# Token scales stored row by row, ternary pieces moved to later units, the second layer's first waits split, and the feed-forward stage run one tile further ahead

## The chip, the cores and the metric

The kernel runs on one core of one Trainium2 chip. What is measured is the device time of one execution, in microseconds (us). Engines are named PE (TensorE matmuls), DVE (VectorE), ACT (ScalarE), POOL (GpSimd) and SP (SyncE, which here only issues DMA transfers).

## The reference, cut

Two transformer layers, batch 4, 1024 tokens, width 512, 16 heads of 32:

```python
# layer 0: all in float32
h = sln(x, cond, ...); q, k, v = h @ Wqkv.T + bqkv
out = (softmax(q k^T) / 512**0.5 @ v) @ Wp.T + bp
h1 = out + x;  x1 = sln(h1, cond, ...) + h1
# layer 1: every linear is a "bitlinear"
act_quant(x):    s = 127 / clip(max|x| over the row); round(x*s) / s
weight_quant(w): s = 1 / clip(mean|w|); clip(round(w*s), -1, 1) / s
bitlinear(x, w, b) = act_quant(x) @ weight_quant(w).T + b
xn = rmsnorm(x1, g1) * (1 + scale) + shift         # scale, shift from bitlinear(c, w_ada1)
x2 = x1 + bitlinear(attention(bitlinear(xn, w_qkv)), w_proj)
h  = gelu(bitlinear(adaln(x2, ada2), w_fc1))
y  = x2 + bitlinear(h, w_fc2)
```

## The kernel before, in words

`build` runs three stages after each other, each with its own buffers, split by barriers: `layer0` (names a_...), `layer1a` (layer 1's attention, b_...) and `layer1b` (the feed-forward part, c_...). A batch is TT = 8 token tiles of 128 rows. Nothing is ordered by a scheduler: each engine's program is written out, and the engines meet at semaphores.

**layer0.** For a batch, PE makes q, k and v in 24 "units" of 512 columns (`UNITS`, 16 for q and k, v = 0 to 15, then 8 for v, 16 to 23), each four float32 products of 512 columns (L766), in four PSUM banks used in turn. From unit 8 (`PRE`) every unit also carries two chunks of the first heads' scores (L332), whose maxima DVE takes (L446, twice a unit). DVE's own part of a unit is the low half of q or k (L1032), or the value tile (L1039), which may be written only once all of the former batch's stored tiles have left their buffer (`s_qout`). Between these, for the batches 1 to 3, DVE does two further jobs, placed by unit number. The first is the former batch's input to layer 1: largest values, scales at unit 9 (`scales`, which makes the token scales `am1[:, 4, :]`, called dq), and eight-bit tiles at units 10 to 13 (`eight_bits`, L988). The second is a quarter of layer 1's ternary weights: `PIECES[b]` are 4 pieces of 2048 columns for batches 2 and 3, and 4 of 1536 and one of 2048 for batch 1; ACT rounds piece j at unit 9 + j (`ROUND_AT`), DVE clips it at unit 10 + j (`TERN_AT`, L1072 and L1074), POOL stores it. After the 24 units come the attention rounds, then a tail (projection, residual, norm). For the last batch scales and eight-bit tiles come after its tail, at the end of the stage.

SP's `quantized(b)` stores the eight tiles (L639), then dq by columns (L641) and dq by rows (L643). The last takes the 128 x 8 table and writes it as 1024 consecutive values, 4 bytes at a time.

**layer1a.** SP issues the loads of the first batch's tiles (xq), its dq (as rows and as columns), the weights w (qkv) and wp (proj), and the biases bqk and bv. w, wp and bqk share the semaphore `s_w`, and PE, ACT, POOL and DVE wait for all three before their first instruction. The first `work` (order `NEXT_ONLY`) transposes the tiles (kind X, four), then makes 16 units of q and k (kind QK). For each, DVE multiplies the product by dq (`dequantized`, L1464), ACT makes the high half (`high`, L1393), and DVE the low half (`low`, L1480), which waits for the high half. The low half follows its own `dequantized` at once for n < `EARLY` = 8. SP then reorders the first heads' q and k by DMA (L256), and DVE takes the first maxima (L446) of products on them.

**layer1b.** N = 32 token tiles go through a software pipeline: `steps` runs a list of (offset, function) for step n, each function on tile n + offset. Steps 1 to 24 run as a loop with four steps in its body, the others are written out before and behind it. A tile goes x_scale (ACT, L1705), modulate, shift, bias (POOL), maximum(0), clipped, inverse, factor (DVE, L1754, L1761, L1767, L1773), x_round (ACT, L1709), x_bits (DVE, L1778), x_transpose (PE, L1655), x_copy (ACT, L1713), fc1 (PE, L1664), hidden (DVE, L1789), gelu (ACT, L1719), maximum(1), clipped, inverse, factor (DVE), h_round (ACT, L1723), h_bits (DVE, L1795), h_transpose (PE, L1673), h_copy (ACT, L1728), fc2 (PE, L1683), residual (DVE, L1801).

## Time and profile before

| what | value |
|---|---|
| median of three runs | 3114.76 us (3105.6 to 3115.96) |
| the profiled execution | 3107.7 us |
| its span, first to last instruction | 3105.5 us |
| mean granted TensorE clock | 0.973 |
| busy: PE, DVE, POOL, ACT | 2840.1, 2244.1, 1999.2, 1788.0 us |

The program's stages, in us from the span's start:

| stretch | stage | PE busy | DVE busy | ACT busy |
|---|---|---|---|---|
| 415 to 506 | units of batch 1 | 87.68 | 60.74 | 32.46 |
| 792 to 884 | units of batch 2 | 87.12 | 59.39 | 31.87 |
| 1170 to 1263 | units of batch 3 | 87.56 | 59.38 | 31.87 |
| 1506 to 1585 | last tail, then eight-bit tiles and stores | 31.42 | 52.76 | 15.65 |
| 1585 to 1651 | layer1a's start | 37.71 | 38.77 | 20.71 |
| 1651 to 2778 | layer1a's attention | 1070.15 | 828.89 | 729.28 |
| 2778 to 3106 | layer1b | 268.46 | 270.56 | 244.75 |

The layer0 attention between these stretches makes up the rest. A stretch in which PE is busy nearly all the time can only be shortened by the little it idles; in the last tail, in layer1a's start and in layer1b it waits for others a good part of the time.

### The profile page before, as it was taken

The page shows a single profiled execution, that of the slowest core. Times are in us where ns is not written, and L with a number is a line of the kernel's source. Part 1 is how long each engine was busy: PE and PEld are TensorE (multiplying, and loading weights), DVE is VectorE, ACT ScalarE, POOL GpSimd, SP SyncE. Part 2 cuts the span into 40 slices and gives each one's busy share as a digit, 9 for nine tenths or more (in the row PEclk, how much of TensorE's full clock was granted, in tenths as well). Part 3 has the DMA queues.
Part 4 walks back from the last instruction along what each step waited for, and adds up shares of the span by engine and source line. Part 5 has one row for each costly group of instructions (what it writes and reads, how often), then busy time and mean ns, then how long its engine had stood idle before and what let it go on. Part 6 is the DMA issues. An engine that isn't in the chain of part 4 may idle for free. (4 is left out here: it accounts for less than half of the span.)

```text
span 3105.5 us, 69316 instructions
## 1 busy us (share of the span) xinstructions
PE 2840.1 (91%) x21927; PEld 1403.9 (45%) x21927; DVE 2244.1 (72%) x4442; ACT 1788.0 (58%) x3210; POOL 1999.2 (64%) x1674
## 2 busy tenths in 40 slices
PE   7999999999999989999739998999899899958898
PEld 5444444444444444445314444454444445524444
DVE  3677686776867777677647777776877687738997
ACT  2366553664546634466325666666666766657887
POOL 0288634886258852588526885888588778854341
PEclk9999999999999999999969999999999999979999
DMA  5022333223422324123031313221422232233000
GB/s 184 22 55 58 140 105 52 52 75 126 112 46 52 115 86 105 42 52 92 35 95 42 77 43 101 57 70 26 111 74 56 51 91 53 46 132 146 30 27 35
DMA packets 99769, 230.62 MB, mean 74 GB/s; under 512 B 22332, under 2 KB 28580, under 8 KB 97960
## 3 DMA queue, kind: packets, MB, share of 16 engines
q1 hardware_dynamic: 97816, 220.90, 25.2%
q0 software_dynamic: 1680, 6.33, 1.3%
q8 instruction: 141, 2.31, 0.3%
q14 instruction: 132, 1.08, 0.1%
HBM read 89.71 MB, written 35.73 MB: 40 GB/s over the span
## 5 line engine op out<-in xcount | busy, mean ns | idle before, releaser
L446 DVE TENSOR_REDUCE b_mxs<-ps 128x1 f32<-128x512 f32 x1024 | 635.4, 682 | 201.0 <-PE ps L332 199.8
L446 DVE TENSOR_REDUCE a_mxs<-ps 128x1 f32<-128x512 f32 x1024 | 635.4, 682 | 183.3 <-PE ps L332 181.9
L417 ACT ACTIVATE b_p<-ps 128x512 f32<-128x512 f32 x1024 | 533.9, 603 | 206.7 <-PE ps L346 201.9
L417 ACT ACTIVATE a_p<-ps 128x512 f32<-128x512 f32 x1024 | 530.6, 602 | 212.1 <-PE ps L346 206.8
L304 POOL TENSOR_TENSOR b_sum<-b_p 128x512 f32<-128x512 f32 x384 | 496.5, 1296 | 87.9 <-ACT b_p L417 87.3
L304 POOL TENSOR_TENSOR a_sum<-a_p 128x512 f32<-128x512 f32 x384 | 498.3, 1301 | 76.9 <-ACT a_p L417 76.8
L332 PE MATMUL ps<-b_k,b_q 96*128 96x512 f32 x1024 | 443.0, 436 | 32.8 <-DVE b_mxs L446 27.0
L332 PE MATMUL ps<-a_k,a_q 96*128 96x512 f32 x1024 | 443.3, 440 | 16.7 <-DVE a_mxs L446 13.2
L346 PE MATMUL ps<-b_q,b_k 98*128 98x512 f32 x1024 | 400.7, 426 | 13.2 <-ACT b_p L417 9.9
L346 PE MATMUL ps<-a_q,a_k 98*128 98x512 f32 x1024 | 397.8, 422 | 14.4 <-ACT a_p L417 14.4
L360 PE MATMUL ps<-a_p,a_vx 128*32 128x512 f32 x2048 | 372.2, 599 | 11.1 <-POOL a_sum L309 9.3
L360 PE MATMUL ps<-b_p,b_vx 128*32 128x512 f32 x2048 | 370.8, 601 | 0.6 <-POOL b_sum L309 0.4
L362 PE MATMUL ps<-a_sum,a_unit 128*32 128x512 f32 x768 | 370.2, 599 | 0.0
L362 PE MATMUL ps<-b_sum,b_unit 128*32 128x512 f32 x768 | 368.9, 601 | 0.0
L309 POOL TENSOR_TENSOR b_sum<-b_sum,b_p 128x512 f32<-128x512 f32 x256 | 328.8, 1284 | 37.5 <-POOL b_sum L304 18.1
L309 POOL TENSOR_TENSOR a_sum<-a_sum,a_p 128x512 f32<-128x512 f32 x256 | 329.4, 1287 | 35.5 <-POOL a_sum L304 16.0
L332 PEld LDWEIGHTS ps<-b_k,b_q 96*128 96x128 f32 x1024 | 198.1, 194 | 214.2 <-issue 104.9
L332 PEld LDWEIGHTS ps<-a_k,a_q 96*128 96x128 f32 x1024 | 194.2, 190 | 210.3 <-issue 121.3
L346 PEld LDWEIGHTS ps<-a_q,a_k 98*128 98x128 f32 x1024 | 192.0, 189 | 145.2 <-ACT a_p L417 98.1
L346 PEld LDWEIGHTS ps<-b_q,b_k 98*128 98x128 f32 x1024 | 194.8, 191 | 128.5 <-ACT b_p L417 84.9
L766 PE MATMUL ps<-a_hT,a_w 128*128 128x512 f32 x512 | 231.1, 604 | 8.4 <-DVE a_hT L919 8.4
L426 ACT ACTIVATE a_ots<-ps 128x512 f32<-128x512 f32 x128 | 76.4, 597 | 132.4 <-PE ps L362 131.9
(220 smaller groups left out, 3888.8 us busy)
## 6 DMA issues: line engine op xcount, KB each, us to landing
a_q<-a_qh SPq DMA_DIRECT2D x128, 128.0 KB, 2.3
a_k<-a_kh SPq DMA_DIRECT2D x128, 128.0 KB, 2.4
b_q<-b_qh SPq DMA_DIRECT2D x128, 128.0 KB, 2.4
b_k<-b_kh SPq DMA_DIRECT2D x128, 128.0 KB, 2.4
a_kl<-in_x SPq DMA_DIRECT2D x4, 2048.0 KB, 8.5
a_q<-a_ql SPq DMA_DIRECT2D x64, 128.0 KB, 2.3
a_k<-a_kl SPq DMA_DIRECT2D x64, 128.0 KB, 2.3
a_kh<-in_x SPq DMA_DIRECT2D x4, 2048.0 KB, 14.4
```

The lines of the kernel that those rows point to most:

```text
L304: pair = pool.tensor_tensor(tile, self.key_tile(u, kt), self.key_tile(u, kt + 1), ALU.add)
L309: pool.tensor_tensor(tile, tile, self.key_tile(u, kt + 2), ALU.add).then_inc(self.s_sum, 1)
L332: pe.matmul(self.mx[RING[at]], self.q[j][0:96, t * P:(t + 1) * P], self.k[j][0:96, half * HALF:(half + 1) * HALF], start=True, stop=True). ...
L346: pe.matmul(self.st[RING[at]], self.k[j][:, kt * P:(kt + 1) * P], self.q[j][:, u * HALF:(u + 1) * HALF], start=True, stop=True).then_inc(s ...
L360: pe.matmul(self.ot[u][HD * c:HD * (c + 1), :], self.vx[k % 2][:, kt, :], self.key_tile(u, kt), start=r == 0, stop=kt + 3 >= TT)
L362: pe.matmul(self.ot[u][3 * HD:4 * HD, :], self.ones[:, :], self.sum[:, at % self.NS, :], start=r == 0, stop=r == self.ROUNDS - 1).then_inc ...
L417: act.activation(self.key_tile(u, kt), self.st[RING[CHUNKS * (k % NJ) + n]], ACT.Exp, scale=self.scale).then_inc(self.s_exp, 1)
L426: act.activation(self.ots[:, u, :], self.ot[u], ACT.Copy).then_inc(self.s_ots, 1)
L446: dve.reduce_max(self.mxs[:, c:c + 1], self.mx[RING[CHUNKS * j + c]], axis=AX.X).then_inc(self.s_mxr, 1)
L766: mm = pe.matmul(ps[:, bank(v), :], lhs, rhs, start=k == 0, stop=k == KC - 1)
```

## The change

It has four parts.

1. **Rows of dq.** PE transposes the 128 x 8 table into a corner of a PSUM bank (`token_scales`, at unit 10 of the next batch, or after the last tail); DVE copies the 8 x 128 result out (`token_rows`, at unit 12, or after the last `scales`); SP stores it as eight rows of 512 bytes. SP waits for the copy ahead of this store. PE's m_transpose at unit 20, which uses the same bank, waits for the copy too.
2. **Later pieces.** In batches 1 to 3 a ternary piece j is rounded at unit 11 + j and clipped at unit 13 + j.
3. **First waits of layer1a.** bqk is loaded second, wp last and with a semaphore of its own, for which PE waits only before the first tail work. PE waits for w and bqk at the first QK product, not before its transposes; ACT at the first high half. In the first round the low half of unit n - 1 follows the dequantization of unit n.
4. **layer1b.** x_scale and POOL's three steps work on tile n + 6 instead of n + 5 while x_round and maximum(0) work on n + 5 (before: n + 4), so a tile has a step between x_scale and x_round. x_scale stands before x_round on ACT. x_bits works on tile n + 4 (before: n + 3) and stands later on DVE. The first x tile is loaded by itself, then the modulation rows and b2, then the other seven, then the weights.

```diff
-        SUM_AT, TOT_AT, INV_AT, ROUND_AT, TERN_AT = 1, 7, 8, 9, 10
+        SUM_AT, TOT_AT, INV_AT, ROUND_AT, TERN_AT = 1, 7, 8, (9, 11, 11, 11), (10, 13, 13, 13)
...
                     sp.dma_start(Pending.dq_col[b, :, :], am1[:, 4, :]).then_inc(s_qout, 16)
-                        sp.dma_start(Pending.dq_row[b, :].rearrange("(t p) -> p t", p=P), am1[:, 4, :]).then_inc(s_qout, 16)
+                    sp.wait_ge(s_dqrow, b + 1)
+                    sp.dma_start(Pending.dq_row[b, :].rearrange("(t p) -> t p", p=P), dq_t[:, :]).then_inc(s_qout, 16)
...
+                def token_scales(b):
+                    pe.wait_ge(s_dq, b + 1)
+                    pe.transpose(dq_ps, am1[:, 4, :], ident).then_inc(s_dqt, 1)
...
+                        if b and v == DQT_AT:
+                            token_scales(b - 1)
                         if v == MT:
                             pe.wait_ge(s_rowse, 1)
+                            if b:
+                                pe.wait_ge(s_dqrow, b)
...
+                def token_rows(b):
+                    dve.wait_ge(s_dqt, b + 1)
+                    if b:
+                        dve.wait_ge(s_qout, OUTS * b)
+                    dve.tensor_copy(dq_t[:, :], dq_ps).then_inc(s_dqrow, 1)
...
-                for dst, src in ((w[:, :, :], wq["qkv"]), (wp[:, :, :], wq["proj"]), (bqk[:, :], ins["b_qk"])):
+                for dst, src in ((w[:, :, :], wq["qkv"]), (bqk[:, :], ins["b_qk"])):
                     sp.dma_start(dst, src).then_inc(s_w, 16)
                 sp.dma_start(bv, rows(ins["b_v"], P)).then_inc(s_bv, 16)
+                sp.dma_start(wp[:, :, :], wq["proj"]).then_inc(s_wp, 16)
...
-                pe.wait_ge(s_w, 16 * 3)
...
+                        if kind == "QK" and n == 0:
+                            pe.wait_ge(s_w, 16 * 2)
...
-                            if kind == "QK" and n < EARLY:
-                                low(n, nxt)
+                            if kind == "QK" and 0 < n <= EARLY and tail is None:
+                                low(n - 1, nxt)
...
-    FIRST, AHEAD = -5, 5
+    FIRST, AHEAD = -6, 6
...
-                steps(pool, ((5, modulate), (5, shift), (5, bias)), all_mod)
+                steps(pool, ((6, modulate), (6, shift), (6, bias)), all_mod)
...
-                steps(act, ((-1, h_copy), (3, x_copy), (0, h_round), (1, gelu), (4, x_round), (5, x_scale)), all_x)
+                steps(act, ((-1, h_copy), (3, x_copy), (0, h_round), (1, gelu), (6, x_scale), (5, x_round)), all_x)
...
-                steps(dve, ((0, maximum(1)), (3, x_bits), (0, clipped(1)), (2, hidden(0)), (0, inverse(1)), (2, hidden(1)),
-                            (0, factor(1)), (4, maximum(0)), (0, h_bits), (4, clipped(0)), (-1, residual), (4, inverse(0)),
-                            (4, factor(0))))
+                steps(dve, ((0, maximum(1)), (0, clipped(1)), (0, inverse(1)), (2, hidden(0)), (2, hidden(1)),
+                            (0, factor(1)), (5, maximum(0)), (4, x_bits), (5, clipped(0)), (0, h_bits), (5, inverse(0)),
+                            (-1, residual), (5, factor(0))))
```

In the lists that follow, a row is one instruction (or several alike, x2): its line, its operation, its output and inputs.

DVE in layer0, units 9 (its end) to 11 of batch 1, before. a_kl and a_ql are a unit's low half, a_mxs its two maxima, a_vx and a_xv eight-bit tiles, a_p and a_sum a ternary piece:

```order
L1032 SCALAR_TENSOR_TENSOR a_kl<-ps,a_bqk,a_kh 128x512
L446 TENSOR_REDUCE a_mxs<-ps 128x1 x2
L988 TENSOR_SCALAR a_vx<-a_xv 128x512
L988 TENSOR_SCALAR a_xv<-a_xv 128x512
L1072 TENSOR_SCALAR a_p<-a_p 128x1536
L1074 TENSOR_SCALAR a_sum<-a_p 128x1536
L1032 SCALAR_TENSOR_TENSOR a_kl<-ps,a_bqk,a_kh 128x512
L446 TENSOR_REDUCE a_mxs<-ps 128x1 x2
L988 TENSOR_SCALAR a_xv<-a_xv 128x512 x2
L1072 TENSOR_SCALAR a_p<-a_p 128x1536
L1074 TENSOR_SCALAR a_p<-a_p 128x1536
```

The same engine after, units 11 to 13 of batch 1 (a_dq_t is the row copy):

```order
L1052 SCALAR_TENSOR_TENSOR a_ql<-ps,a_bqk,a_qh 128x512
L446 TENSOR_REDUCE a_mxs<-ps 128x1 x2
L1008 TENSOR_SCALAR a_xv<-a_xv 128x512 x2
L1002 COPY a_dq_t<-ps 8x128
L1052 SCALAR_TENSOR_TENSOR a_ql<-ps,a_bqk,a_qh 128x512
L446 TENSOR_REDUCE a_mxs<-ps 128x1 x2
L1008 TENSOR_SCALAR a_xv<-a_xv 128x512 x2
L1094 TENSOR_SCALAR a_p<-a_p 128x1536
L1096 TENSOR_SCALAR a_sum<-a_p 128x1536
```

The first ternary piece moved from the unit of the first eight-bit tiles to that of the last ones, and the small copy stands one unit ahead of it.

DVE at layer1a's start, before (b_qh<-ps is a dequantization, b_ql<-b_qh and b_kl<-b_ql a low half):

```order
L1464 TENSOR_TENSOR b_qh<-ps,b_dqr 128x512
L1480 SCALAR_TENSOR_TENSOR b_ql<-b_qh,b_bqk 128x512
L1464 TENSOR_TENSOR b_qh<-ps,b_dqr 128x512
L1480 SCALAR_TENSOR_TENSOR b_ql<-b_qh,b_bqk 128x512
L1464 TENSOR_TENSOR b_ql<-ps,b_dqr 128x512
L1480 SCALAR_TENSOR_TENSOR b_kl<-b_ql,b_bqk,b_kh 128x512
```

And after:

```order
L1492 TENSOR_TENSOR b_qh<-ps,b_dqr 128x512 x2
L1508 SCALAR_TENSOR_TENSOR b_ql<-b_qh,b_bqk 128x512
L1492 TENSOR_TENSOR b_ql<-ps,b_dqr 128x512
L1508 SCALAR_TENSOR_TENSOR b_ql<-b_qh,b_bqk 128x512
L1492 TENSOR_TENSOR b_ql<-ps,b_dqr 128x512
L1508 SCALAR_TENSOR_TENSOR b_kl<-b_ql,b_bqk,b_kh 128x512
```

Each low half now has the next unit's dequantization ahead of it.

One step of layer1b's loop on DVE, before (c_tk is a tile of x, c_h a tile of the hidden layer):

```order
L1754 TENSOR_REDUCE c_am<-c_h 128x1
L1778 TENSOR_SCALAR c_xq<-c_tk 128x512
L1761 TENSOR_SCALAR c_am<-c_am 128x1
L1789 SCALAR_TENSOR_TENSOR c_h<-ps,c_am,c_b 128x1024
L1767 RECIPROCAL c_am<-c_am 128x1
L1789 SCALAR_TENSOR_TENSOR c_h<-ps,c_am,c_b 128x1024
L1773 TENSOR_SCALAR c_am<-c_am,c_wsc 128x1
L1754 TENSOR_REDUCE c_am<-c_tk 128x1
L1795 TENSOR_SCALAR c_hq<-c_h 128x2048
L1761 TENSOR_SCALAR c_am<-c_am 128x1
L1801 SCALAR_TENSOR_TENSOR c_x<-ps,c_am,c_x 128x512
L1767 RECIPROCAL c_am<-c_am 128x1
```

And after:

```order
L1790 TENSOR_REDUCE c_am<-c_h 128x1
L1797 TENSOR_SCALAR c_am<-c_am 128x1
L1803 RECIPROCAL c_am<-c_am 128x1
L1825 SCALAR_TENSOR_TENSOR c_h<-ps,c_am,c_b 128x1024 x2
L1809 TENSOR_SCALAR c_am<-c_am,c_wsc 128x1
L1790 TENSOR_REDUCE c_am<-c_tk 128x1
L1814 TENSOR_SCALAR c_xq<-c_tk 128x512
L1797 TENSOR_SCALAR c_am<-c_am 128x1
L1831 TENSOR_SCALAR c_hq<-c_h 128x2048
L1803 RECIPROCAL c_am<-c_am 128x1
L1837 SCALAR_TENSOR_TENSOR c_x<-ps,c_am,c_x 128x512
L1809 TENSOR_SCALAR c_am<-c_am,c_wsc 128x1
```

The x bits moved from right behind the first maximum to behind the second, and three small operations on the hidden tile's maximum now follow each other instead of standing between long ones.

The same step on ACT, before and then after:

```order
L1728 ACTIVATE c_hT<-ps 128x1024 x2
L1713 ACTIVATE c_xqT<-ps 128x512
L1723 ACTIVATE c_h<-c_h,c_am 128x2048
L1719 ACTIVATE c_h<-c_h 128x1024 x2
L1709 ACTIVATE c_tk<-c_tk,c_am 128x512
L1705 ACTIVATE c_tk<-c_x,c_rs 128x512
```

```order
L1764 ACTIVATE c_hT<-ps 128x1024 x2
L1749 ACTIVATE c_xqT<-ps 128x512
L1759 ACTIVATE c_h<-c_h,c_am 128x2048
L1755 ACTIVATE c_h<-c_h 128x1024 x2
L1741 ACTIVATE c_tk<-c_x,c_rs 128x512
L1745 ACTIVATE c_tk<-c_tk,c_am 128x512
```

The scale of a later tile and the rounding of an earlier one changed places, and the rounding now stands right ahead of h_copy.

## Rows read from the trace of the kernel before

**Rows 1.** Timeline of PE, layer0: start, length, line, shapes; starts around units 8 and 22.

```profile
439.57 2.82 PE L766 MATMUL ps<-a_hT,a_w 128*128 128x512 f32 x6
...
498.16 1.02 PE L766 MATMUL ps<-a_w,a_hT 128*128 128x512 f32 x2
...
816.13 3.68 PE L766 MATMUL ps<-a_hT,a_w 128*128 128x512 f32 x8
...
872.67 3.60 PE L766 MATMUL ps<-a_w,a_hT 128*128 128x512 f32 x8
...
876.57 3.60 PE L766 MATMUL ps<-a_w,a_hT 128*128 128x512 f32 x8
...
1194.52 3.68 PE L766 MATMUL ps<-a_hT,a_w 128*128 128x512 f32 x8
...
1257.57 4.88 PE L766 MATMUL ps<-a_w,a_hT 128*128 128x512 f32 x11
```

**Rows 2.** Timeline of DVE, units of batch 2; brackets: idle before, what ended it.

```profile
834.07 0.74 DVE L1032 SCALAR_TENSOR_TENSOR a_kl<-ps,a_bqk,a_kh 128x512 fp32r<-128x512 f32 x1
...
836.79 1.22 DVE L1072 TENSOR_SCALAR a_p<-a_p 128x2048 f32<-128x2048 f32 x1
...
839.19 0.74 DVE L1032 SCALAR_TENSOR_TENSOR a_ql<-ps,a_bqk,a_qh 128x512 fp32r<-128x512 f32 x1
...
859.17 0.69 DVE L1039 TENSOR_TENSOR a_xv<-ps,a_bv 128x512 f32<-128x512 f32 x1 [5.33 <-DMA dq_row<-a_am]
```

**Rows 3.** DMA issues, 1555 to 1600 us: count, KB each, median us to landing.

```profile
xq<-a_xv SPq DMA_DIRECT2D x7, 128.0 KB, 1.9
...
dq_row<-a_am SPq DMA_DIRECT2D x1, 4.0 KB, 10.1
```

**Rows 4.** Timeline of SP's queue at layer1a's start: the issue of wp, bqk, first reordering loads.

```profile
1586.77 0.64 SPq L1279 DMA_DIRECT2D b_wp<-wq_proj  x1
1587.45 0.43 SPq L1279 DMA_DIRECT2D b_bqk<-in_b_qk  x1
...
1612.57 1.21 SPq L256 DMA_DIRECT2D b_q<-b_qh  x2
```

**Rows 5.** Timeline of PE, then POOL, at layer1a's start.

```profile
1597.77 3.57 PE L1325 MATMUL ps<-identb,b_kh 128*128 128x128 bf16 x32 [59.09 <-DMA b_bqk<-in_b_qk]
1602.73 5.34 PE L1337 MATMUL ps<-b_xqT,b_w 128*128 128x512 bf16 x24 [1.39 <-ACT b_xqT L1386]
...
1590.26 0.09 POOL L199 MEMSET b_fold<- 1x1 f32 x1
```

**Rows 6.** Timeline of DVE, layer1a's start: the first low half, the first maxima.

```profile
1605.34 0.75 DVE L1480 SCALAR_TENSOR_TENSOR b_ql<-b_qh,b_bqk 128x512 fp32r<-128x512 f32 x1 [0.79 <-ACT b_qh L1393]
...
1622.78 1.28 DVE L446 TENSOR_REDUCE b_mxs<-ps 128x1 f32<-128x512 f32 x2
```

**Rows 7.** Timelines of PE and of ACT, layer1b: one early tile, then the loop.

```profile
2820.89 1.06 PE L1673 MATMUL ps<-identb,c_hq 128*128 128x128 bf16 x16
...
2913.94 1.90 PE L1683 MATMUL ps<-c_w,c_hT 128*128 128x512 bf16 x8 [0.93 <-ACT c_hT L1728]
...
2921.08 1.06 PE L1673 MATMUL ps<-identb,c_hq 128*128 128x128 bf16 x16
...
2821.53 1.94 ACT L1728 ACTIVATE c_hT<-ps 128x1024 bf16<-128x1024 bf16 x2 [1.78 <-PE ps L1673]
...
2912.88 1.91 ACT L1728 ACTIVATE c_hT<-ps 128x1024 bf16<-128x1024 bf16 x2
...
2920.77 0.72 ACT L1709 ACTIVATE c_tk<-c_tk,c_am 128x512 f32<-128x512 f32 x1 [0.29 <-DVE c_am L1767]
```

**Rows 8.** x_bits and h_bits by tile, ns min/median/max; then POOL's timeline in the loop.

```profile
L1778 DVE TENSOR_SCALAR c_xq<-c_tk x32: 414/1018/1070, 2794.6 to 3069.0; 128x512 bf16<-128x512 f32 x32
...
L1795 DVE TENSOR_SCALAR c_hq<-c_h x32: 1226/1227/1228, 2816.7 to 3094.7; 128x2048 bf16<-128x2048 f32 x32
...
2922.32 1.26 POOL L1637 TENSOR_TENSOR c_tk<-c_tk,c_mod_r 128x512 f32<-128x512 f32 x1 [5.17 <-ACT c_tk L1705]
```

More of the change, by code:

```diff
@@ L641, in quantized @@
                     sp.dma_start(Pending.dq_col[b, :, :], am1[:, 4, :]).then_inc(s_qout, 16)
-                    with nc.allow_non_contiguous_dma(reason="1024 values a batch"):
-                        sp.dma_start(Pending.dq_row[b, :].rearrange("(t p) -> p t", p=P), am1[:, 4, :]).then_inc(s_qout, 16)
+                    sp.wait_ge(s_dqrow, b + 1)
+                    sp.dma_start(Pending.dq_row[b, :].rearrange("(t p) -> t p", p=P), dq_t[:, :]).then_inc(s_qout, 16)
                 def batch(b, last):
@@ L808, in batch @@
                         front(b + 1, b)
+                    else:
+                        pe.wait_ge(s_h1, TT * (b + 1))
+                        token_scales(b)
                 batches(pe, first, batch)
@@ L1141, in batch @@
                         chn.close()
+                        token_rows(b)
                         for t in range(TT):
@@ L1359, in work @@
                         pe.wait_ge(s_qf, UN * nxt + EARLY)
+                    if tail is not None:
+                        pe.wait_ge(s_wp, 16)
                     for kind, n, bank, before, part in order:
@@ L1389, in high @@
                     m, c = UNITS[n]
+                    if n == 0:
+                        act.wait_ge(s_w, 16 * 2)
                     act.wait_ge(s_qf, UN * nxt + n + 1)
@@ L1605, in _ @@
                 for b in range(B):
-                    sp.dma_start(x[:, TT * b:TT * (b + 1), :],
-                                 x_in[b * T:(b + 1) * T, :].rearrange("(t p) d -> p t d", p=P)).then_inc(s_x[b], 16)
-                    sp.dma_start(mod_r[:, b, :, :].rearrange("p i d -> p (i d)"),
-                                 rows(mod[b, :, :].rearrange("i d -> (i d)"), P)).then_inc(s_mod[b], 16)
-                    if b == 0:
-                        sp.dma_start(b2[:, :], rows(ins["b_fc2"], P)).then_inc(s_b2, 16)
+                    for lo, hi in ((0, 1), (1, TT)) if b == 0 else ((0, TT),):
+                        sp.dma_start(x[:, TT * b + lo:TT * b + hi, :],
+                                     x_in[b * T + lo * P:b * T + hi * P, :].rearrange("(t p) d -> p t d", p=P)).then_inc(s_x[b] if hi == TT else s_x0, 16)
+                        if (b, lo) == (0, 0):
+                            sp.dma_start(mod_r[:, b, :, :].rearrange("p i d -> p (i d)"),
+                                         rows(mod[b, :, :].rearrange("i d -> (i d)"), P)).then_inc(s_mod[b], 16)
+                            sp.dma_start(b2[:, :], rows(ins["b_fc2"], P)).then_inc(s_b2, 16)
+                    if b:
+                        sp.dma_start(mod_r[:, b, :, :].rearrange("p i d -> p (i d)"),
+                                     rows(mod[b, :, :].rearrange("i d -> (i d)"), P)).then_inc(s_mod[b], 16)
+                    else:
                         sp.dma_start(w1[:, :, :], wq["fc1"]).then_inc(s_w1, 16)
@@ L1695, in _ @@
                 act.wait_ge(s_rs, 1)
[L1696 removed]
+                act.wait_ge(s_x0, 16)
                 def all_x():
@@ L1702, in x_scale @@
                 def x_scale(n, r):
+                    if isinstance(n, int) and n == 1:
+                        act.wait_ge(s_x[0], 16)
                     if not isinstance(n, int) or n >= 2:
```

20 lines of the change are left out of this document (12 added, 8 removed).

## The prediction

> **What bounds the kernel now.** I read first the table of stages: PE is busy for nearly all of the attention and of layer0's units, and idles mainly in three places, the last tail with layer1a's start (1506 to 1651) and layer1b (268.46 of 328 us). The change touches these three and the units of the batches 1 to 3. Then I read the timelines there. In the units, PE runs one unit in 3.90 us when nothing holds it (872.67 to 876.57 [rows 1]); DVE needs 5.12 for a unit that carries a ternary piece of 2048 (834.07 to 839.19), 2.40 of it for the piece (836.79 to 839.19), and stands 5.33 before the first value tile until the row store of dq has landed [rows 2]. At the end of layer0 nothing runs but that store [rows 3]. At layer1a's start PE waits for the bias load [rows 5], and then DVE stands 0.79 before each low half until ACT has made the high half [rows 6]. In layer1b's loop PE idles 0.93 a tile before fc2, and ACT, which makes fc2's input, idles 0.29 before x_round for DVE's inverse [rows 7].
>
> About 0.3% of this time, 9.3 us, is what a measurement of this kernel can tell from no change; the chances use that bound.
>
> **Units of layer0 (parts 1 and 2).** From unit 8 to unit 22 PE took 439.57 to 498.16 = 58.6, 816.13 to 876.57 = 60.4 and 1194.52 to 1257.57 = 63.1 [rows 1]. Fourteen units at 3.90 are 54.6, so 4.0 + 5.8 + 8.5 = 18.3 are lost. Two things lose it: DVE's overloaded units (eight-bit tiles and a ternary piece in the same unit), and the wait for the store at unit 16. The store leaves after the last eight-bit tile and lands 10.1 after its issue, where a tile of 128 KB, written by rows, takes 1.9 [rows 3]. A store of eight 512-byte rows is no more work than that, so I take 1.9 and the wait of 5.33 goes, with its smaller or larger fellows in the other two batches. The bounds are 1.7 (the column store stands just below the tile's) and 10.1, where nothing would be gained; the last is a rival. The pieces now meet only one unit that has eight-bit tiles, unit 13, and then units 14 to 16 with nothing else. Unit 13 still takes 5.1 as in rows 2, and 14 and 15 take 5.12 less two eight-bit operations (about 0.4 each), 4.3. So 1.2 + 0.4 + 0.4 stay lost beyond 3.90, less what four banks of slack cover: I estimate 1.3 in each of the batches 2 and 3, none in batch 1 with its smaller pieces. Added are three transposes of 128 x 8 on PE: sixteen bf16 ones take 1.06 [rows 7], so 0.07 is the low end for one, and the first score chunk's 0.5 is more than one can take; I take 0.1, near the low end, as it is one small product, 0.4 in all with its wait. DVE's copy of 8 x 128 takes a small operation's time, beside a unit that has lost its ternary piece: nothing. If that cover were gone it would cost 0.2 to 0.7 (a low half) each. The new wait of PE at unit 20 is for a copy at unit 12: nothing. Queued behind SP's new wait is only the row store itself, and the wait ends at unit 12, while the last eight-bit tile, ahead of it in the queue, is made at unit 13. POOL's stores of the weights are issued two or three units later: DVE clips the last piece at unit 16 (17 in batch 1), POOL's attention work waits for the value tiles at 23, so nobody waits. The sum is 18.3 - 2.6 - 0.4 = **15.3**, between 10 (half of the overload stays) and 18.
>
> **End of layer0 (part 1).** The row store lands 10.1 after issue and layer1a starts behind it. With 1.9 it starts **8.2** earlier. The transpose and the copy there stand ahead of the first eight-bit tile on DVE, but those are paced by ACT's rounding, so they cost nothing or, without that cover, under 0.7. The bounds are 7 and 8.4.
>
> **layer1a's start (part 3).** PE began its transposes at 1597.77, released by the bias (issued 1587.45), and the first product at 1602.73, 4.96 later [rows 4, 5]. POOL's setup ends at 1590.35 [rows 5]; from there transposes and their copies put the first product at 1595.3. The bias, now issued where wp stood (1586.77, 0.68 earlier), would release PE at 1597.1, and wp's 512 KB no longer lie ahead of it, for which I take 0.9, half of what the transposes leave. That is 1596.2. The later decides: 1602.7 - 1596.2 = **6.5**, between 4 (nothing from wp's bytes, and the first products at the low clock, twice as long for their first 1.6) and 7.4 (the transposes decide). Behind it, DVE's low halves. From the first, 1605.34, to the first maxima, 1622.78, lie 17.4 with eight low halves, each behind an idle 0.79 [rows 6]. With the next dequantization between, the high half is ready. Eight by 0.79 is 6.3, less 0.2 for the first low half now one operation later: **6.1**. If instead the reordering loads set the time (issued 1612.57 [rows 4], after the fourth low half), only the first four count, 2.7.  I take the upper value, since the maxima come 10 us after those loads' issue, which no transfer in rows 3 takes when it has the queue to itself except the 4-byte one. Sum 12.6, between 7 and 14.
>
> **layer1b (part 4).** The period is 9.13 a tile: fc2 at 2913.94, h_transpose at 2921.08, its 1.06 and the idle 0.93 give the next fc2 at 2923.07. It closes through ACT: h_copy at 2912.88 to fc2 at 2913.94 is 1.06; fc2 to h_transpose, PE working without a gap, 2913.94 to 2921.08 is 7.14; and a copy that waits for its transposes starts 0.64 after them (2820.89 to 2821.53) [rows 7]. The sum is 8.84. In the loop the copy starts later than these 0.64, because x_round and x_scale stand ahead of it and x_round waited 0.29 for DVE. After the change x_scale, which waits for nobody in this step, fills that wait, so ACT's own loop is 9.13 - 0.29 = 8.84 too. Gain 0.29 x 24 loop steps = 7.0, with the steps written out around the loop about **7.3**. It needs DVE to be done in 8.84: its operations sum to about 8.1 with x_bits at the 0.41 that it takes away from POOL's stretch (its minimum, against a median of 1.02 [rows 8]), and with three dependent small operations in a row now, some 0.13 dearer each. The first tile alone makes the first x_scale earlier, but fc1 of tile 0 waits for w1, whose place in the queue hardly moved: 0 to 1. The bounds are 0 (a rival) and 12, should PE's 8.20 of own work set the period, 0.93 x 13.
>
> **Sum.** 15.3 + 8.2 + 12.6 + 7.3 = 43.4 off the profiled execution's 3107.7 (span 3105.5 and 2.2 around it) gives 3064.3. The median of the runs lies 7.1 above that execution; I add half, since runs of either kind occur: **3067.8**.
>
> **Rivals.**
> *The feed-forward period stays (0.15).* DVE's chain of dependent small operations, or x_round now right ahead of h_copy and behind an inverse that DVE makes after h_bits, takes the place of the wait removed. Against it: 0.7 us of slack on DVE. Then 7.3 is missing, or up to 6 more (0.25 a step) is lost: 3075 to 3081.
> *layer1a's start gains little (0.12).* Weights land no earlier, and the loads set the maxima: 4 + 2.7 instead of 12.6, 3073.7. For it speaks that transfers there share the engines.
> *The row store is no quicker (0.04).* Then 8.2 and about 7.5 of the units' gain are missing: 3083.5. Against it: both tile and column stores take under 2.
> *Slower (0.02).* h_bits, 1.227 us in every tile now [rows 8], falls into POOL's stretch of three operations. x_bits, which lies in it, takes 1.02 against 0.41, 2.5 times as long; h_bits would take 3.0, 1.8 more, and DVE, at 8.1 + 1.8 = 9.9, becomes the bound: 0.8 a step over 9.13, in 31 steps 24, and if residual and hidden are pushed into that stretch behind it 51. The latter costs more than all the gains: 3119. It decides if POOL's stretch starts some 2.4 us later against h_bits than its place behind x_scale says; x_scale follows two gelu operations of 1 us each on ACT, so it starts when h_bits has ended. This is the weakest of the cases.
> The Trainium skill, in "SBUF — State Buffer", section "Who interferes with whom", states that DVE and GpSimd contend only for a shared port pair, as an exclusive lock. By that the later engine waits out at most one instruction of the other, and the time lost doesn't grow with the length of its own. The rows above can't tell lock from slowing: 0.6 lost beside a POOL operation of 1.26 [rows 8] fits both. By the lock the overlap would cost at most one such operation a step, 1.27 x 31 = 39, and this rival would end at about 3107, no longer slower; I give that outcome 0.01.
>
> **Chances.** The forecast as it stands 0.66, the rivals as given (0.15, 0.12, 0.04, 0.02, 0.01). Faster by over 0.3% is all but the last two: 0.96, with 0.02 for no change and 0.02 for slower. The range takes the first three rivals' middle in and the unknown costs above: low 3054 (units 18, end 8.4, start 14, layer1b 9, and a median run equal to the profiled one), high 3084.
>
> **What would show it.** In the changed profile: PE units 8 to 22 in 54.6 to 57; no wait of DVE for dq_row before the value tiles; the row store landing in about 1.9; PE's first product in layer1a some 15 us earlier in the span than the units' gain alone says, and the first maxima about 14 after it, where it was 20; in the loop of layer1b a period of 8.84, x_bits at 0.41 and h_bits still at 1.227. The forecast is wrong if a transfer at layer1a's start takes longer because its neighbours moved, or if x_round waits for DVE in the loop again.

## The result, and the profile after

The changed kernel ran in 3070.38 us (median of four, 3068.01 to 3078.25), the kernel before in 3113.95 (four, 3105.6 to 3115.96). The ratio is 0.9869, 95% interval 0.9844 to 0.9895. A second series on one chip gave 0.9877 (0.9858 to 0.9895). 3067.8 had been forecast.

The profiled execution of the changed kernel is its slowest, 3078.25 us with a span of 3076.5; that of before was a quick one of its kind, 3107.7 us with a span of 3105.5. So between the two traces lie only 29.0, between the medians 43.6: the one lies 7.9 above its median, the other 6.3 below. The time is therefore followed below by stages.

The page's busy times after:

```profile
PE 2852.6 (93%) x21931; PEld 1415.0 (46%) x21931; DVE 2239.3 (73%) x4446; ACT 1791.2 (58%) x3210; POOL 1998.3 (65%) x1674
```

**Units of layer0.** PE's timeline in batch 2, the starts of units 8 and 22, and between them the only piece where it still waits (start, length, line, shapes, idle before and what ended it):

```profile
813.08 3.68 PE L773 MATMUL ps<-a_hT,a_w 128*128 128x512 f32 x8
...
852.77 0.50 PE L332 MATMUL ps<-a_k,a_q 96*128 96x512 f32 x1 [0.47 <-DVE a_mxs L446]
...
869.11 7.03 PE L773 MATMUL ps<-a_w,a_hT 128*128 128x512 f32 x16
```

They answer to [rows 1]: 56.0 where it was 60.4. Batch 1 takes 55.0 (58.6 before), batch 3 56.1 (63.1). DVE's first value tile no longer waits for a store, against 5.33 in [rows 2]:

```profile
851.44 0.68 DVE L1059 TENSOR_TENSOR a_xv<-ps,a_bv 128x512 f32<-128x512 f32 x1
```

**End of layer0, start of layer1a.** SP's queue: the row store, and the next stage's first load 2.92 behind it, where a store alone took 10.1 to land [rows 3]; then the first reordering load.

```profile
1561.44 0.34 SPq L646 DMA_DIRECT2D dq_row<-a_dq_t  x1
1564.36 0.35 SPq L1272 DMA_DIRECT2D b_kh<-xq  x1
...
1566.37 0.44 SPq L1302 DMA_DIRECT2D b_bqk<-in_b_qk  x1
...
1584.48 1.20 SPq L256 DMA_DIRECT2D b_q<-b_qh  x2
```

PE there, answering to [rows 5]: its transposes are released by POOL's setup, its first product by the bias, and the first score chunk now waits for a reordering load.

```profile
1570.53 3.57 PE L1348 MATMUL ps<-identb,b_kh 128*128 128x128 bf16 x32 [15.07 <-POOL b_fold L199]
1575.69 10.47 PE L1362 MATMUL ps<-b_xqT,b_w 128*128 128x512 bf16 x40 [1.58 <-DMA b_bqk<-in_b_qk]
...
1590.06 1.22 PE L332 MATMUL ps<-b_k,b_q 96*128 96x512 f32 x2 [2.69 <-DMA b_k<-b_kh]
```

DVE, answering to [rows 6]: the first low half has no idle before it, and the first maxima come 15.2 after the first product, where it was 20.05 (1602.73 to 1622.78).

```profile
1579.89 0.74 DVE L1508 SCALAR_TENSOR_TENSOR b_ql<-b_qh,b_bqk 128x512 fp32r<-128x512 f32 x1
...
1590.89 1.29 DVE L446 TENSOR_REDUCE b_mxs<-ps 128x1 f32<-128x512 f32 x2 [0.24 <-PE ps L332]
```

**layer1b.** One step of the loop on PE, answering to [rows 7]:

```profile
2889.66 1.90 PE L1717 MATMUL ps<-c_w,c_hT 128*128 128x512 bf16 x8 [0.67 <-ACT c_hT L1764]
...
2896.80 1.06 PE L1707 MATMUL ps<-identb,c_hq 128*128 128x128 bf16 x16
2898.53 1.90 PE L1717 MATMUL ps<-c_w,c_hT 128*128 128x512 bf16 x8 [0.67 <-ACT c_hT L1764]
```

And x_bits by its tile (ns minimum/median/maximum), answering to [rows 8]:

```profile
L1814 DVE TENSOR_SCALAR c_xq<-c_tk x32: 412/416/869, 2772.2 to 3034.6; 128x512 bf16<-128x512 f32 x32
```

The period is 8.87, where it was 9.13, and PE's idle before fc2 is 0.67 instead of 0.93.

### The profile page after: what moved, and what is told of

It reads as the page before. It is cut to its first block and busy times, and to the rows that moved or that the text cites. A ratio compares the mean times of both kernels' runs of the same rounds, so it can differ in the third digit from the quotient of the medians.

```text
span 3076.5 us, 69328 instructions
## 1 busy us (share of the span) xinstructions
PE 2852.6 (93%) x21931; PEld 1415.0 (46%) x21931; DVE 2239.3 (73%) x4446; ACT 1791.2 (58%) x3210; POOL 1998.3 (65%) x1674
```

## The experiments

All kernels are compared stage by stage in their traces, since single executions of one kernel differ by 10 us within a series and by more between chips, more than most parts are worth. Every column of this table is a difference of two starts on PE: from unit 8 to unit 22 in batches 1, 2, 3; from one product in the last tail (the one at 1520.07 in the first trace) to layer1a's first product; from that to the 14th score product; from the 40th score product to the last one of layer1a (work that no edit touches); the mean step of layer1b over 24 steps.

| kernel | units | tail to product | to 14th | attention | period |
|---|---|---|---|---|---|
| before | 58.6 60.4 63.1 | 82.7 | 29.9 | 1058.9 | 9.135 |
| after | 55.0 56.0 56.1 | 67.3 | 26.8 | 1064.2 | 8.870 |
| e1_rows | 56.9 58.8 58.7 | 74.0 | 31.9 | 1059.7 | 9.136 |
| e2_pieces | 59.3 59.0 59.5 | 83.9 | 32.0 | 1059.3 | 9.135 |
| e3_waits | 59.9 64.8 65.9 | 77.8 | 30.3 | 1059.0 | 9.137 |
| e3_low | 61.5 64.9 65.2 | 84.3 | 26.5 | 1059.4 | 9.136 |
| e4_swap | 60.0 64.8 65.2 | 84.3 | 32.1 | 1059.6 | 9.161 |
| e9_inverse | 58.3 60.0 62.3 | 82.7 | 30.2 | 1061.7 | 8.906 |
| e8_xbits_in | 55.0 56.1 56.0 | 67.4 | 26.9 | 1062.8 | 8.870 |
| after_again | 55.0 56.1 56.1 | 67.3 | 26.8 | 1062.8 | 8.870 |
| e5_xfirst | 55.0 56.1 56.1 | 67.6 | 25.6 | 1061.8 | 8.646 |
| e6_fc1split | 55.0 56.1 56.1 | 67.6 | 26.5 | 1062.8 | 8.446 |
| e7_dve | 55.0 56.1 56.1 | 67.8 | 26.4 | 1064.4 | 8.328 |
| best | 55.0 55.2 55.5 | 67.3 | 25.2 | 1058.9 | 8.329 |

The kernels with e in their name are single executions on several chips, and each chip has a time of the kernel before: e1_rows, e2_pieces, e3_waits and e4_swap ran where it took 3123.09, e3_low, e5_xfirst, e6_fc1split and e7_dve where it took 3122.1, e9_inverse where it took 3104.8, and e8_xbits_in, after_again and best on the chip of the second series. Of these, e1_rows took 3092.8, e2_pieces 3113.61, e3_waits 3112.86, e3_low 3118.68, e4_swap 3121.77, e5_xfirst 3060.92, e6_fc1split 3062.62, e7_dve 3062.81 and e8_xbits_in 3072.37.

### Which of parts 1 and 2 shortens the units

e1_rows is the kernel before with part 1 alone, e2_pieces with part 2 alone:

```diff
# e1_rows, against the kernel before: dq stored by rows
+                    sp.wait_ge(s_dqrow, b + 1)
+                    sp.dma_start(Pending.dq_row[b, :].rearrange("(t p) -> t p", p=P), dq_t[:, :]).then_inc(s_qout, 16)
# e2_pieces, against the kernel before
-        SUM_AT, TOT_AT, INV_AT, ROUND_AT, TERN_AT = 1, 7, 8, 9, 10
+        SUM_AT, TOT_AT, INV_AT, ROUND_AT, TERN_AT = 1, 7, 8, (9, 11, 11, 11), (10, 13, 13, 13)
```

> The kernel before with the row store alone changed (transpose, copy, eight rows), ternary pieces where they were. PE took 58.6, 60.4 and 63.1 us from unit 8 to unit 22 in batches 1, 2, 3, and 55.0, 56.0 and 56.1 after the whole change. Theory, that the wait for the store costs most and the overloaded units a part of their own: about 55.5, 57.5 and 57.5, and layer1a starts 8.2 earlier against the last tail. Rival, that the store's wait explains all of it: 55.0, 56.0, 56.1 as with the whole change. Rival, that the overload explains all: above 58 in each.

> The kernel before with the ternary pieces at units 13 and later alone, dq stored 4 bytes at a time. Theory: the first lag (units 10 to 13) goes, about 1 us a batch, the wait of DVE for the store stays: 57.5, 59.5 and 60 us from unit 8 to unit 22. If the store's wait were all: 58.6, 60.4, 63.1 unchanged. If the pieces were all: 55, 56, 56. Layer1a's start doesn't move against the last tail.

Sums over the three batches: 182.1 before (180.6 to 191.5 in the five traces whose layer0 is as before), 174.5 with the rows, 177.8 with the pieces, 167.1 with both. So neither explains it alone. The fair comparison is with the traces from the same chip: e3_waits and e4_swap, whose layer0 is as before, show 190.6 and 190.1 there. Against them the rows alone bring about 16, the pieces alone about 12.5 and both about 23, so the two overlap; against the first trace, where the old store landed sooner, the same kernels would seem to bring only 7.6 and 4.3. With the rows alone, the wait for the store is gone, but PE waits for DVE's maxima three times in batch 2:

```profile
838.54 0.50 PE L332 MATMUL ps<-a_k,a_q 96*128 96x512 f32 x1 [0.85 <-DVE a_mxs L446]
...
843.98 0.50 PE L332 MATMUL ps<-a_k,a_q 96*128 96x512 f32 x1 [1.27 <-DVE a_mxs L446]
...
849.10 0.50 PE L332 MATMUL ps<-a_k,a_q 96*128 96x512 f32 x1 [0.95 <-DVE a_mxs L446]
```

With the pieces alone DVE fills part of the wait with the moved pieces, and what is left of it still holds PE:

```profile
857.91 0.69 DVE L1039 TENSOR_TENSOR a_xv<-ps,a_bv 128x512 f32<-128x512 f32 x1 [1.38 <-DMA dq_row<-a_am]
...
859.26 0.50 PE L332 MATMUL ps<-a_k,a_q 96*128 96x512 f32 x1 [2.09 <-DVE a_mxs L446]
```

e1_rows also moved layer1a's first product by 8.7 against the trace of before and 10.3 against e4_swap, whose row store landed later; e2_pieces (83.9) didn't move it beyond what the old store does by itself (82.7 to 84.3). I had put e1_rows at 55.5, 57.5 and 57.5: each was 1.2 to 1.4 more, so the overload costs more than I thought. e2_pieces came within 0.5 of the expected 59.5 and 60 in batches 2 and 3, and 1.8 over the 57.5 of batch 1.

The units with the old store varied between traces, those with both parts didn't (55.0 in batch 1 in all seven, 167.1 or 167.2 in sum in the six with the same pieces). The wait is longer on some chips; batch 2 of e4_swap, DVE, against 5.33 in [rows 2]:

```profile
860.26 0.69 DVE L1039 TENSOR_TENSOR a_xv<-ps,a_bv 128x512 f32<-128x512 f32 x1 [6.75 <-DMA dq_row<-a_am]
```

There the store took 12.6 to land, 11.1 in batch 2 of the first trace, which is the 1.4 by which the wait grew. The other 3.0 of the 4.4 that the stretch is longer are PE's own busy time, at a granted clock of 0.94 over 816 to 877, where it was 1.00 in the first trace (windows: stretch, length, PE, PEld, DVE, ACT and POOL busy, then PEclk):

```profile
816.00:877.00 61.00, 55.13 (x132) 25.62 (x132) 42.00 (x72) 17.79 (x21) 5.11 (x6) 0.94 0.33 59
```

### layer1a's first waits and the low halves, apart

```diff
# e3_waits, against the kernel before (loads: w, bqk, bv, then wp with its own semaphore)
-                pe.wait_ge(s_w, 16 * 3)
...
+                        if kind == "QK" and n == 0:
+                            pe.wait_ge(s_w, 16 * 2)
# e3_low, against the kernel before
-                            if kind == "QK" and n < EARLY:
-                                low(n, nxt)
+                            if kind == "QK" and 0 < n <= EARLY and tail is None:
+                                low(n - 1, nxt)
```

> The kernel before with layer1a's loads and first waits alone changed; the low half stays right behind its own dequantization. Theory: PE's first q or k product comes 6.5 to 7 earlier after the stage's first load is issued (it was 17.9 after, 11.3 with the whole change), and the first maxima 20 after that product, as before. Rival, that the early product is taken back by the reordering loads: maxima 21.5 or more after the product.

> The kernel before with layer1a's low halves alone moved behind the next dequantization; loads and first waits as before. From the first q or k product to a fixed product after the first eight units PE took 32.3 us in the first trace of the kernel before, 34.3 to 34.5 in the kernels of the first call with that order, 29.2 after the change. Theory, that the order of the low halves gives this part, and then the reordering loads set the first chunk: 29 to 30, the first chunk waits 2 to 3 for a load. Rival, that the early weights are needed too: 31 or more.

The waits alone bring 6.5 (84.3 in e4_swap and e3_low, 77.8 here), and the 14th score product comes 30.3 after the first product, as without the edit. On the mark of the expectation, which leaves out how long the row store took, the first product comes 11.3 after the stage's first load with the new waits (in the changed kernel as well), where it was 17.9 before and 18.0 in e4_swap; the first maxima come 20.1 after the product, as expected. The low halves alone bring the 14th score product to 26.5 after the first product, as with the whole change, where six traces with the old order show 29.9 to 32.1: 3.4 to 5.6. (The expectation named a mark a little later in the program, where the same difference is seen.) What sorts the six is the granted clock of the first products, as the account of the low halves below shows. The two edits don't depend on each other. That the loads are next is seen in the changed kernel's first score chunk above, idle 2.69 for one of them, and 2.71 in e3_low.

### What holds layer1b's loop

```diff
# e4_swap, against the kernel before
-                steps(act, ((-1, h_copy), (3, x_copy), (0, h_round), (1, gelu), (4, x_round), (5, x_scale)), all_x)
+                steps(act, ((-1, h_copy), (3, x_copy), (0, h_round), (1, gelu), (5, x_scale), (4, x_round)), all_x)
```

> The kernel before with x_scale (tile n + 5) and x_round (tile n + 4) exchanged on ACT alone, no tile further ahead, DVE's order and the first loads as before. Theory, that only ACT's wait of 0.29 between gelu and x_round held the loop: the period falls from 9.13 to 8.86, all that the change in layer1b brings, with x_bits still at 1.02. Rival, that it needs x_bits out of POOL's stretch or the tile further ahead: 9.0 to 9.13.

The period became 9.161: nothing gained. ACT no longer waits at x_round, but it now waits 0.35 ahead of h_round:

```profile
2930.49 2.00 ACT L1723 ACTIVATE c_h<-c_h,c_am 128x2048 f32<-128x2048 f32 x1 [0.35 <-DVE c_am L1767]
```

DVE and POOL of the same step show why: POOL's stretch begins earlier against DVE, x_bits starts 0.09 after POOL's second operation and takes 1.46, and the inverse for which h_round waits stands behind it and behind hidden(0).

```profile
2927.57 1.46 DVE L1778 TENSOR_SCALAR c_xq<-c_tk 128x512 bf16<-128x512 f32 x1
2928.95 0.14 DVE L1761 TENSOR_SCALAR c_am<-c_am  x1
2929.02 1.27 DVE L1789 SCALAR_TENSOR_TENSOR c_h<-ps,c_am,c_b 128x1024 f32<-128x1024 f32 x1
2930.21 0.14 DVE L1767 RECIPROCAL c_am<-c_am  x1
...
2927.48 1.27 POOL L1641 TENSOR_TENSOR c_tk<-c_tk,c_mod_r 128x512 f32<-128x512 f32 x1 [0.18 <-POOL c_tk L1637]
2928.70 1.46 POOL L1644 TENSOR_TENSOR c_x<-c_x,c_b 128x512 f32 x1
```

Two candidates were left: x_bits' length and the inverse's place. e8_xbits_in is the changed kernel with x_bits back behind the first maximum, e9_inverse is e4_swap with inverse(1) ahead of hidden(0), with no tile further ahead:

```diff
# e8_xbits_in, against the changed kernel
-                steps(dve, ((0, maximum(1)), (0, clipped(1)), (0, inverse(1)), (2, hidden(0)), (2, hidden(1)),
-                            (0, factor(1)), (5, maximum(0)), (4, x_bits), (5, clipped(0)), ...
+                steps(dve, ((0, maximum(1)), (4, x_bits), (0, clipped(1)), (0, inverse(1)), (2, hidden(0)), (2, hidden(1)),
+                            (0, factor(1)), (5, maximum(0)), (5, clipped(0)), ...
# e9_inverse, against e4_swap
-                steps(dve, ((0, maximum(1)), (3, x_bits), (0, clipped(1)), (2, hidden(0)), (0, inverse(1)), (2, hidden(1)),
+                steps(dve, ((0, maximum(1)), (3, x_bits), (0, clipped(1)), (0, inverse(1)), (2, hidden(0)), (2, hidden(1)),
```

> The changed kernel with x_bits put back right behind the first maximum on DVE, where it meets POOL's three operations; tile offsets and ACT's order stay. Theory, that x_bits waits out the POOL operation that is under way: it takes 1.0 to 1.5 instead of 0.41, DVE, which fills 8.65 of the 8.87, becomes the bound, and the period is 9.2 to 9.5. Rival, that the tile further ahead and ACT's order were what mattered: 8.87.

> The kernel before with x_scale and x_round exchanged on ACT (as in the run that gave 9.161 and x_bits at 1.45) and with inverse(1) ahead of hidden(0) on DVE; no tile further ahead. Theory, that in that run ACT's h_round waited 0.35 for the inverse behind hidden(0), and that x_bits' place doesn't matter: h_round doesn't wait, the period is 8.87 as after the whole change. Rival, that x_bits at 1.45 fills DVE: its work from one h_bits to the next is 8.9 there without the idle 0.27, and with dependent gaps the period stays at 9.0 to 9.15, so that the tile further ahead is what lets x_bits leave.

e8_xbits_in kept 8.870, against my theory: x_bits took 0.65 to 0.90 in the loop's steps (a median of 0.77 over all), since it began in the second half of a POOL operation, and DVE had room for that. e9_inverse came to 8.906, with most steps at 8.87 and no wait ahead of h_round:

```profile
2915.54 1.17 DVE L1778 TENSOR_SCALAR c_xq<-c_tk 128x512 bf16<-128x512 f32 x1
...
2917.86 1.99 ACT L1723 ACTIVATE c_h<-c_h,c_am 128x2048 f32<-128x2048 f32 x1
```

So of part 4 the exchange on ACT together with inverse(1) ahead of hidden(0) makes nearly all of it, 0.23 of the 0.265 a step. Whether inverse(1)'s new place would do without the exchange no run shows. By e8_xbits_in the new place of x_bits adds nothing, so the remaining 0.04 belong to the tile further ahead with the rest of DVE's new order. In these two single runs e9_inverse and the kernel before took 3104.67 and 3104.8; its loop is 6 us shorter by its trace, but that is within what one execution of each can show.

### What holds it after the change

```diff
# e5_xfirst, against the changed kernel
-                steps(pe, ((-1, fc2(0)), (3, x_transpose), (-1, fc2(1)), (3, fc1), (0, h_transpose)), ...
+                steps(pe, ((3, x_transpose), (-1, fc2(0)), (-1, fc2(1)), (3, fc1), (0, h_transpose)), ...
# e6_fc1split: moreover
+                steps(pe, (..., (3, fc1((0, 1, 2))), (0, h_transpose), (3, fc1((3,)))), ...
# e7_dve: moreover
-                steps(dve, ((0, maximum(1)), (0, clipped(1)), (0, inverse(1)), (2, hidden(0)), (2, hidden(1)),
-                            (0, factor(1)), (5, maximum(0)), ...
+                steps(dve, ((0, maximum(1)), (0, clipped(1)), (0, factor(1)), (0, inverse(1)), (2, hidden(0)), (2, hidden(1)),
+                            (5, maximum(0)), ...
```

> The changed kernel with x_transpose ahead of the first half of fc2 on PE. Theory, that PE's loop over h_copy closes at 8.86 (7.14 from fc2 to h_transpose, 0.64 and 1.06 around the copy) and that x_transpose can use PE's idle 0.67: the loop is 0.22 shorter, and DVE, whose work and dependent gaps fill about 8.65, becomes the bound: period 8.65. Rival, that DVE or POOL already sets 8.87: unchanged 8.87.

> The changed kernel with x_transpose first and the last of fc1's four banks behind h_transpose, so that PE has work while ACT copies. PE's loop over the copy would be 7.75, PE's own work 8.20. Theory, that DVE is then the bound: 8.6 to 8.65, no better than x_transpose first alone. Rival, that PE's loop was the only bound: 8.2 to 8.3.

> As the kernel with fc1 split, and on DVE factor(1) stands between clipped(1) and inverse(1), so that one dependent pair of small operations is parted. If DVE is the bound, the period falls by 0.12 to 0.2, to 8.45 to 8.5. If it isn't, it stays as with fc1 split alone.

The periods are 8.646, 8.446 and 8.328. e5_xfirst is as expected: the four small transposes moved into PE's idle stretch, and the loop over h_copy became 0.22 shorter. But that was still PE's loop, not DVE: e6_fc1split, where PE never waits for the copy, went 0.2 lower. I had read DVE's filled time as 8.65 and it is 8.45; some of its gaps were waits that went along. In e6_fc1split DVE is the bound: ACT waits for two of its inverses in a step, and PE waits 0.38 for h_bits.

```profile
2906.49 0.72 ACT L1747 ACTIVATE c_tk<-c_tk,c_am 128x512 f32<-128x512 f32 x1 [0.51 <-DVE c_am L1805]
...
2910.06 2.01 ACT L1761 ACTIVATE c_h<-c_h,c_am 128x2048 f32<-128x2048 f32 x1 [0.53 <-DVE c_am L1805]
...
2915.00 1.06 PE L1709 MATMUL ps<-identb,c_hq 128*128 128x128 bf16 x16 [0.38 <-DVE c_hq L1833]
```

Parting one pair of dependent small operations took 0.118 off the period: inverse(1) starts 0.30 after clipped(1) in e6_fc1split with nothing between them, and 0.29 after it in e7_dve with factor(1) between them. So factor(1) costs nothing there, where it took 0.12 behind the hidden operations.

### The changed kernel again, and a quicker one

```diff
# best, against the changed kernel: e7_dve's orders, and
-        ... ROUND_AT, TERN_AT = 1, 7, 8, (9, 11, 11, 11), (10, 13, 13, 13)
+        ... ROUND_AT, TERN_AT = 1, 7, 8, (9, 11, 12, 12), (10, 13, 14, 14)
...
-                            if kind == "QK" and 0 < n <= EARLY and tail is None:
+                            if kind == "QK" and 0 < n <= EARLY and n != 4 and tail is None:
                                 low(n - 1, nxt)
+                            if kind == "QK" and n == 3 and tail is None:
+                                low(n, nxt)
...
-                    for lo, hi in ((0, 1), (1, TT)) if b == 0 else ((0, TT),):
+                    for lo, hi in ((0, 2), (2, TT)) if b == 0 else ((0, TT),):
...
+                            sp.dma_start(w1[:, :, :], wq["fc1"]).then_inc(s_w1, 16)    # now ahead of the other six tiles
```

> The changed kernel once more. If the 5 us that layer1a's attention took longer in its first trace (1164.9 against 1157.9 to 1159.1 from its 40th score product to the first h_transpose) come from TensorE's granted clock and not from an edit, they differ again here. Units 55.0, 56.05, 56.1, the period of layer1b 8.87. Ratio to the kernel before 0.985 to 0.988.

> The changed kernel with x_transpose first, fc1 split and the parted small operations (period 8.33 instead of 8.87, 13 us), the pieces of batches 2 and 3 one unit later (56.05 to 55.1, 2 us), the fourth low half ahead of the fifth dequantization in layer1a (0.4), and in layer1b two x tiles loaded first and w1 ahead of the other six (its first transpose 2 to 5 us earlier). In all 17 to 21 faster than the changed kernel in the same call: ratio to the kernel before 0.979 to 0.982.

On one chip, three rounds each: the changed kernel 3073.32 (3065.98 to 3076.37), best 3048.19 (3045.59 to 3052.29), before 3109.7 (3107.37 to 3113.53). Ratios to before: 0.9877 (0.9858 to 0.9895) and 0.9805 (0.9789 to 0.9822). best is 25 faster than the changed kernel, where 17 to 21 had been expected: by the traces, 16.3 from the first h_transpose to the end (13.0 in the loop as reckoned, 3.3 in the steps around it), 1.4 from the units (167.1 to 165.7), 1.6 to the 14th score product, where the kernels with the changed start already spread from 25.6 to 26.8, and the rest is within the spread of the medians. In layer1b its first transpose came 20.9 after PE's last product of layer1a, against 21.8, where I had hoped for 2 to 5; the same distance is 20.8 in e1_rows, whose layer1b is the old one, and up to 23.2 in others, so nothing is shown to be gained.

```profile
2757.85 0.58 PE L1691 MATMUL ps<-identb,c_xq 128*128 128x128 bf16 x4 [20.56 <-DVE c_xq L1818]
```

after_again answers only a part of the question where the other 15 us of the first pair of traces are. I had expected its layer1a attention to differ from the 1064.2 of the first trace; it took 1062.8, nearly the same. best, whose attention is the same program, took 1058.9, so the edits don't make the longer time necessary. But six of the seven traces with the first three parts show 1061.8 to 1064.4 and the seven others 1058.9 to 1061.7: whether the change makes it likelier stays open. What the time consists of is seen: for the same products PE was busy 1024.86 in the first trace after, 1018.86 before and 1019.07 in best, at a mean granted clock of 0.98 against 0.99. One stretch of it, at the change of a batch in layer1a (after, then best, 56 us each from like places):

```profile
1870.00:1926.00 56.00, 47.14 (x194) 24.85 (x193) 45.55 (x86) 32.99 (x57) 28.10 (x24) 0.82 0.40 117
```

```profile
1864.00:1920.00 56.00, 46.13 (x209) 23.88 (x208) 46.62 (x83) 35.64 (x63) 31.93 (x28) 0.88 0.38 111
```

## Why the prediction was right, point by point

**Units (15.3 forecast).** 58.6 + 60.4 + 63.1 less 55.0 + 56.0 + 56.1 is 15.0. Both causes were there, and the residue was 1.0 in batches 2 and 3 where I took 1.3, none in batch 1. It comes from unit 13 and its neighbours, as the reckoning said: with the pieces one unit later it is 0.1 and 0.5. The smaller residue hides that every batch stays 0.4 over the 54.6 of 14 free units, where I had put 0.4 for the three transpositions together; one takes 0.27 on PE. Against the three traces in which the store was slower (190.1 to 191.5) the gain is 23 to 24, which the profiled pair couldn't show: I had reckoned with one value of a wait that varies.

**Given back behind the units.** From unit 22 to a point some 20 us into the attention the first trace lost 1.4, 1.5 and 1.6 in the three batches, which no step of mine had. The granted clock of that stretch was 0.86 (869 to 894) in the changed kernel and 1.00 in e5_xfirst, which is the same program up to there and lost nothing:

```profile
869.00:894.00 25.00, 22.98 (x85) 12.10 (x84) 14.30 (x26) 10.83 (x20) 12.52 (x12) 0.86 0.14 30
```

```profile
869.00:894.00 25.00, 22.33 (x124) 10.81 (x126) 15.44 (x29) 12.13 (x23) 13.93 (x13) 1.00 0.15 35
```

PE idled 0.86 and 1.16 there in either, as before the change. The kernels without the change have such stretches too (0.93 behind batch 1 in the first trace of before, 0.86 in e9_inverse behind batch 3), so it doesn't take the edits to bring them about. What makes one execution fall to the lower level (1.2 GHz) and the other stay at 2.4 stays open.

**End of layer0 and first product (8.2 + 6.5).** Together 15.4 instead of 14.7. In the two traces the stage's first load comes 2.92 after the row store's issue instead of 11.69, 8.8 less, and the first product 11.3 after that load instead of 17.9, 6.6 less. The first is above my bound of 8.4: the old store landed 10.14 after its issue, 1.55 ahead of the load, so the new one took some 1.4, an estimate from 2.92 less 1.55, since its landing isn't in the trace. The bias did decide the first product, landing at 1566.37 + 9.2, and POOL's setup the transposes.

**Low halves (6.1).** In this pair of traces the first maxima came 4.85 earlier against the first product, and by the 14th score product 3.1 were left. What I reckoned on DVE came out: from the start of the first low half to that of the eighth lay 14.98 (1605.34 to 1620.32), and now lie 8.83 (1579.89 to 1588.72), 6.15 less. The term that was wrong is the 0.2 for the first low half's later place. It starts 4.20 after the first product, where it was 2.61, because those first products ran at a lower granted clock: the first dequantization starts 1.96 after the first product instead of 1.13, and the second, now ahead of the low half, waits 0.95 for PE (the first 5 us of products before, then after; DVE after):

```profile
1602.73:1607.73 5.00, 5.00 (x24) 2.23 (x24) 2.30 (x4) 1.44 (x2) 0.00 (x0) 1.00 0.01 3
```

```profile
1575.69:1580.69 5.00, 5.00 (x16) 1.94 (x17) 2.10 (x4) 1.40 (x2) 0.00 (x0) 0.66 0.21 82
```

```profile
1579.29 0.69 DVE L1492 TENSOR_TENSOR b_qh<-ps,b_dqr 128x512 f32<-128x512 f32 x1 [0.95 <-PE ps L1362]
```

The other traces part this from the edit. With the old order, the three with a clock of 1.00 here (before, e3_waits, e9_inverse) have the first maxima 20.1 and the 14th score product 29.9 to 30.3 after the first product; the three with 0.58 to 0.63 (e1_rows, e2_pieces, e4_swap) have 20.9 and 31.9 to 32.1. The eight kernels with the new order all had 0.61 to 0.71 here, and 14.8 to 15.3 for the maxima. At a like clock, e3_low (0.66) against e4_swap (0.58), the new order brings 6.0 at the maxima, as forecast, and 5.6 at the 14th score product. So the upper value was the right choice over the bound by the reordering loads, though PE's first chunk now waits 2.69 for one. The new first waits don't bring the low clock by themselves, since e3_waits had 1.00; whether the change makes it likelier stays open.

**layer1b (7.3).** From the first h_transpose to the end 284.65 became 277.20, 7.5 less; the period is 8.87 for the 8.84 forecast. x_bits fell to 0.42 (its median) and h_bits stayed at 1.227. The size was right. The mechanism was half right: that the loop over h_copy closes at 8.84 is borne out by e5_xfirst, where 0.22 less in that loop took 0.22 off the period. That x_scale in the place of the wait would do it is refuted by e4_swap: there the wait of 0.29 came back as one of 0.35 ahead of h_round, for the other inverse. What the reckoning lacked is that moving x_scale moves POOL's stretch against DVE, and that inverse(1) had to leave its place behind hidden(0). I had counted that move as a cost only, so that the change contained it is luck. DVE's slack was 0.4 and not 0.7, since e6_fc1split shows it as the bound at 8.446. The first tile by itself brought nothing (21.8 from layer1a's last product to the first transpose in both, and 20.8 to 22.7 in the other kernels with the old layer1b): x_scale of tile 1, which waits for the other tiles, stands ahead of x_round of tile 0.

**The rivals.** None came. The slower one rested on h_bits growing in proportion, 2.5 times, if it met POOL. Wherever x_bits met one, it took what was left of the POOL operation under way plus about 0.3: 1.02 with 0.74 left (before), 1.46 with 1.18 left (e4_swap), 1.17 with 0.90 left (e9_inverse), 0.65 with 0.37 left (e8_xbits_in). The operation that follows on POOL took 1.46 instead of 1.27 in the steps of the last three. For x_bits that is waiting, and not slowing, and its cost is bounded by one POOL operation. If the same holds for h_bits, which no run started beside a POOL operation, that rival could not have reached 51.
This is what the Trainium skill says in "SBUF — State Buffer", section "Who interferes with whom" (an exclusive lock, by which the later engine fully blocks for the other's instruction). The trace agrees for x_bits; I should have given its outcome more weight than the proportional one.

**The sum.** It gave 43.4 for the profiled pair, which shows 29.0, and 43.6 between the medians. The parts that edits touch add up to 15.0 + 15.4 + 3.1 + 7.5 = 41.0; 4.5 behind the units and 5.3 in layer1a's attention were given back at the lower clock, which leaves 31.2, and small shifts make the rest. I had taken the profiled execution of before as quick and added half of the difference, 3.5; it came out within 2.6 of the median. That closeness is partly luck: the units' gain depends on how slow the old store is, by 8, the low halves lost 1 to 2.5 to the clock, and no step of mine had the clock at all. The low end of the range was also added up wrongly: its terms, 18 + 8.4 + 14 + 9, taken off 3107.7 give 3058 and not 3054.

## What to carry to other kernels

A loop that closes over several engines has several loops of nearly the same length: exchange two operations in one and look where the wait turns up on the others, above all where POOL's work lands against DVE's. Order an engine's list so that the results others wait for come first, and put independent small operations between dependent ones.
A store of many 4-byte pieces is worth a transpose and a copy wherever its landing is waited for. Where a profiled execution is not a typical one, sum by stages and not by the total.
